# Small softmax vectors moved to the small buffers, and 256 bytes put in front of the query, key and output weights

## The chip, the cores and the metric

The kernel runs on one core of a Trainium2 chip. The metric is the device time of one execution in microseconds (us), launch to end, as the median of several executions.

## What is computed

An input x of 32 batches, 32 tokens each, 512 features, passes through one transformer layer with a per-batch condition. Cut to what matters:

```python
H, KV, HD, HID = 32, 8, 128, 512             # 32 query heads, 8 key/value heads
h = einsum('bct,bcd->bdt', x, W[cond])       # mixes the 32 tokens of a batch
q, k, v = h @ wq, h @ wk, h @ wv             # then rotary embedding on q and k
att = softmax(mask(q @ k.T / sqrt(HD)))      # 32 x 32 scores per batch and head
x = x + (att @ v) @ wo                       # wo: 4096 x 512
y = einsum('bct,bcd->bdt', x, W2[cond])
x = x + quantize(quantize(y) @ qweight.T * scale + bias)
```

All of it is float32. The 1024 rows (32 batches times 32 tokens) are 8 tiles of 128 rows.

## The kernel before

**Precision.** TensorE gets float32 matrices as pairs of "float32r" parts, a high part (`_hi`, made by ScalarE) and what is left over (`_lo`, made by GpSimd or VectorE). `three_pass` multiplies such pairs by three matmuls of 512 columns each into the same PSUM bank; each instruction loads its own 128 x 128 stationary operand:

```python
for i, ((l_hi, l_lo), (r_hi, r_lo)) in enumerate(pairs):
    pe.matmul(dst, l_hi, r_hi, start=(i == 0), stop=False)           # L721
    pe.matmul(dst, l_hi, r_lo, start=False, stop=False)              # L722
    mm = pe.matmul(dst, l_lo, r_hi, start=False, stop=(i == n - 1))  # L723
```

The second argument is stationary (loaded as weights), the third is moving (streamed, 512 float32 values in each partition, 2048 bytes). In a row of the profile, `bank<-A,B` names the moving operand and then the stationary one, without buffer numbers, so `wo7_hi` appears as `wo_hi` and `o2_hi` as `o_hi`.

**Stages.** Everything is written by hand for each engine, and the engines meet only in semaphores. (1) Opening: the conditions are selected, h is computed, and `values` (L693 to L695) computes v for all rows in 16 units of 12 matmuls: units 0 to 7 with `wo_hi`/`wo_lo` as the moving buffers (they hold half of wv then), units 8 to 15 with `o_hi`/`o_lo` as moving buffers. The stationary operand is `hT_hi`/`hT_lo` in all 16. (2) Steady part: for each key/value head g (0 to 7) and each half h (0, 1) of the work, TensorE runs `attend` (small matmuls `p_tr`, `v_st`, L786), `key` (12 matmuls, weights `wk_*`, moving `hT_*`), seven products (`product`, 6 matmuls each, weights `wq_*`, moving `hT_*` or `t_*`: a Strassen-like scheme for two query heads at once), and `project_out` (12 matmuls each for j = 0 to 3, stationary `o_hi`/`o_lo`, moving `wo_hi`/`wo_lo`). In half 1 the small `scores` matmuls (L775) stand between `project_out` j = 2 and j = 3. The heads 2 to 6 are a loop, with g = 0, 1 and 7 written out. (3) Tail: the last projections take other buffers (`wo7_*` moving, `o2_*` or `o_*` stationary), then comes the quantized feed-forward layer in bf16 (L921) with filler matmuls (`hold_clock`, L901).

**Beside TensorE in the steady part.** VectorE (DVE) sums products (`block_sum`, L1021 to L1036), does the two multiplications of the rotary embedding (`rope`, L1045, L1046), softmax (`soft`, L1062 to L1081), the low part of the attention output (`o_low`, L1087) and `accumulate` (L1094), which adds a finished projection to `xacc`. ScalarE (ACT) makes high parts and the half-swapped copy for the rotary embedding (`swap`, L513, L514). GpSimd (POOL) makes low parts of weights and finishes the rotary embedding (`rope_add`, L385). `scores` waits until `rope_add` has finished the fourth query item of the half; `project_out` number n waits until `accumulate` number n - 2 is done.

**Where buffers lie.** `sb` takes the next free bytes of each partition; every buffer begins where the one before it ends, at a multiple of 32 bytes. Buffers of an inner `ExitStack` (`products`, and in it `opening` and `steady`) begin behind those of the outer one. Since nearly all large buffers are multiples of 2048 bytes long, the few small ones set where all that follow begin. This is where the operands of the float32r matmuls begin in a partition, as the remainder of the address divided by 512 (every slice that a matmul takes of them is a whole number of 512 bytes further on):

| buffers | before | after the change |
|---|---|---|
| hT_*, t_*, o_*, o2_*, wo7_* | 64 | 256 |
| wq_*, wk_*, wo_* | 256 | 0 |

So the distance of the stationary operand's start from the moving operand's start, modulo 512, is:

| matmuls | before | after |
|---|---|---|
| products and keys (moving hT, t; stationary wq, wk) | 192 | 256 |
| project_out up to head 6, values units 0 to 7 (moving wo; stationary o, o2, hT) | 320 | 256 |
| values units 8 to 15 (moving o; stationary hT) | 0 | 0 |
| project_out of head 7 (moving wo7; stationary o, o2) | 0 | 0 |

w_sum, s_exp, p_tr and v_st stay where they are. q_rot, k_rot, q_swap, s_nat and the other buffers between hT and o_lo move by 192 bytes together with hT.

Of the kernel before, what the change touches and what calls it, by code (L numbers as in the profile page):

```python
# [7 lines left out]
F32 = mybir.dt.float32  # L8
# [7 lines left out]
P = 128  # L16
# [3 lines left out]
REP = HEADS // KV  # L20
# [5 lines left out]
TPU = TILES // 2  # L26
# [52 lines left out]
def build(nc, x, itok, conds, wq, wk, wv, wo, qweight, w_scale, bias, consts, v_mem, out):  # L79
    with ExitStack() as ctx:  # L80
        def sb(name, shape, dt=F32, area=ctx):
            return area.enter_context(nc.sbuf_tensor(name, shape, dt))
# [10 lines left out]
        y_max = sb("y_max", [P, TILES])  # L93
        f_max = sb("f_max", [P, TILES])
        col = sb("col", [P, 12])
        ones_r = sb("ones_r", [BIAS_ROWS, P], F32R)


        with ExitStack() as products:
            hT_hi = sb("hT_hi", [P, KC, ROWS], F32R, products)  # L100
            hT_lo = sb("hT_lo", [P, KC, ROWS], F32R, products)
            t_hi = sb("t_hi", [P, 4, 2, HALF], F32R, products)
            t_lo = sb("t_lo", [P, 4, 2, HALF], F32R, products)


            with ExitStack() as opening:
                h_full = sb("h_full", [P, KC, ROWS], F32, opening)
                t_full = sb("t_full", [P, 4, 2, HALF], F32, opening)
                selectors = sb("selectors", [P, TILES // 2, 4, 2 * BPT, T], F32, opening)
                wbd1 = sb("wbd1", [P, TILES, BPT, T], F32, opening)  # L110
                wcond = sb("wcond", [P, 4, 2 * T], F32, opening)
                tok_i = sb("tok_i", [P, BATCH], I32, opening)
                tok_f = sb("tok_f", [P, BATCH], F32, opening)
                tok_eq = sb("tok_eq", [P, 4, BATCH], F32, opening)
                warm = sb("warm", [P, 512], BF16, opening)

            with ExitStack() as steady:
                q_rot = sb("q_rot", [P, 2, REP, HALF], F32, steady)
                k_rot = sb("k_rot", [P, 2, HALF], F32, steady)
                q_swap = [sb(f"q_swap{i}", [P, HALF], F32, steady) for i in range(2)]  # L120
                first_p, second_u, third_u = (sb(n, [P, HALF], F32, steady) for n in ("first_p", "second_u", "third_u"))
                s_nat = [sb(f"s_nat{i}", [P, TPU * REP, T], F32, steady) for i in range(2)]
                o_hi = sb("o_hi", [P, TPU, REP * P], F32R, steady)
                o_lo = sb("o_lo", [P, TPU, REP * P], F32R, steady)
                s_max = sb("s_max", [P, TPU * REP], F32, steady)
                s_sum = sb("s_sum", [P, TPU * REP], F32, steady)
                s_rec = sb("s_rec", [P, TPU * REP], F32, steady)
                w_sum = sb("w_sum", [P, 4, 2, HD], F32, steady)
                s_exp = sb("s_exp", [P, TPU * REP, T], F32, steady)
                p_tr = sb("p_tr", [P, TPU * REP, T], F32, steady)  # L130
                v_st = [sb(f"v_st{i}", [P, TPU, HD], F32, steady) for i in range(2)]
                wq_hi = sb("wq_hi", [P, PRODUCTS, 2, HD], F32R, steady)
                wq_lo = sb("wq_lo", [P, PRODUCTS, 2, HD], F32R, steady)
                wk_hi = sb("wk_hi", [P, KC, HD], F32R, steady)
                wk_lo = sb("wk_lo", [P, KC, HD], F32R, steady)
                wo_hi = sb("wo_hi", [P, REP, HID], F32R, steady)
                wo_lo = sb("wo_lo", [P, REP, HID], F32R, steady)
                raw_q = sb("raw_q", [P, 2, KC, 2 * HD], F32, steady)
                raw_k = sb("raw_k", [P, KC, HD], F32, steady)
                raw_o = sb("raw_o", [P, REP, HID], F32, steady)  # L140
# [1194 lines left out]
```

## Time and profile before

| what | value |
|---|---|
| three executions | 546.47, 550.50, 550.77 us; median 550.5 us |
| the profiled execution | 551.23 us, of which its span is 549.4 us |
| busy share of the span: TensorE, VectorE, GpSimd, ScalarE | 94%, 77%, 57%, 46% |
| mean granted share of TensorE's clock | 0.972 |

A row of the profile gives an instruction's start, its duration, and in brackets how long its engine stood idle before it and what ended that. TensorE's instructions overlap, so what one of them costs is not its duration but the distance from its start to the next one's start. Below, that distance is called a step.

### The profile page before, as it was taken

What the parts mean: (1) busy time and instruction counts of PE and PEld (TensorE: products, weight loads), DVE (VectorE), ACT (ScalarE), POOL (GpSimd) and SP (SyncE); (2) the same over time, 40 slices, a digit from 0 to 9 for tenths busy, and PEclk for the clock granted to TensorE, in tenths of its full rate; (3) what the DMA queues carried; (4) which work ended last, traced back from release to release, by engine and by line L of the source; (5) the groups of instructions that cost most, each with busy time, mean ns of one, the idle gap of its engine ahead of it and who ended that gap; (6) DMA issues with size and microseconds to landing.
All of it is one profiled execution on the core that took longest, in us unless ns stands there. A gap on an engine that the chain in (4) does not pass through costs nothing.

```text
span 549.4 us, 9239 instructions
## 1 busy us (share of the span) xinstructions
PE 515.3 (94%) x3150; PEld 407.5 (74%) x3150; DVE 422.1 (77%) x660; ACT 251.2 (46%) x477; POOL 312.6 (57%) x310
## 2 busy tenths in 40 slices
PE   8997999849999999999999999999999999799990
PEld 6886888638787878787888888887878787578530
DVE  5454667696787978797879788887978788765797
ACT  2434256256264636463555446354636453123424
POOL 1247668869838774875688568847884654000002
PEclk9999899978999999999999999999999999989996
DMA  8317311302042022104010401041200023000004
GB/s 262 122 39 245 118 40 38 116 0 58 10 146 57 1 80 75 57 0 153 0 57 0 153 0 57 0 153 34 89 30 20 1 82 116 0 2 1 0 0 153
DMA packets 32644, 35.27 MB, mean 64 GB/s; under 512 B 2251, under 2 KB 22859, under 8 KB 32620
## 3 DMA queue, kind: packets, MB, share of 16 engines
q1 hardware_dynamic: 32620, 34.96, 19.7%
q8 instruction: 14, 0.23, 0.2%
q14 instruction: 10, 0.08, 0.0%
HBM read 28.66 MB, written 6.29 MB: 64 GB/s over the span
## 4 chain that ended last, share of the span: by engine, by line
PE 88%; DVE 5%; POOL 2%; issue 2%; DMA 2%; ACT 1%; SPq 0%; DVEq 0%; ACTq 0%
PE bank L721 24%; PE bank L723 23%; PE bank L722 23%; PE bank L786 3%; PE bank L775 3%; DMA values<-v_st 2%; PE bank L693 2%; PE bank L695 1%; PE bank L694 1%; PE bank L664 1%; PE bank L844 1%; PE bank L921 1%; POOL o_lo L392 1%; PE bank L652 1%; PE bank L901 1%
## 5 line engine op out<-in xcount | busy, mean ns | idle before, releaser
L385 POOL TENSOR_TENSOR q_rot<-q_rot,q_swap 128x512 f32<-128x512 f32 x64 | 88.2, 1378 | 57.9 <-DVE q_swap L1046 57.9
L721 PE MATMUL bank<-wo_hi,o_hi 128*128 128x512 f32 x256 | 103.8, 405 | 3.5 <-issue 3.5
L722 PE MATMUL bank<-wo_lo,o_hi 128*128 128x512 f32 x256 | 102.1, 399 | 0.0
L723 PE MATMUL bank<-wo_hi,o_lo 128*128 128x512 f32 x256 | 102.0, 398 | 0.0
L513 ACT ACTIVATE q_swap<-bank 64x512 f32<-64x512 f32 x80 | 47.6, 596 | 81.7 <-PE bank L723 35.5
L1094 DVE TENSOR_TENSOR xacc<-xacc,bank 128x512 f32<-128x512 f32 x64 | 43.8, 684 | 42.8 <-PE bank L723 42.3
L530 ACT ACTIVATE o_hi<-bank 128x512 fp32r<-128x512 f32 x64 | 33.0, 604 | 73.2 <-PE bank L786 73.2
L721 PEld LDWEIGHTS bank<-wo_hi,o_hi 128*128 128x128 f32 x256 | 48.7, 190 | 17.2 <-issue 5.5
L1046 DVE TENSOR_TENSOR q_swap<-q_swap,cst 128x512 f32<-128x512 f32 x80 | 61.4, 767 | 0.0
L723 PEld LDWEIGHTS bank<-wo_hi,o_lo 128*128 128x128 f32 x256 | 48.8, 191 | 11.9
L722 PEld LDWEIGHTS bank<-wo_lo,o_hi 128*128 128x128 f32 x256 | 48.8, 191 | 10.8
L385 POOL TENSOR_TENSOR k_rot<-k_rot,q_swap 128x512 f32<-128x512 f32 x16 | 20.8, 1298 | 55.4 <-DVE q_swap L1046 55.4
L723 PE MATMUL bank<-t_hi,wq_lo 128*128 128x512 f32 x128 | 50.2, 392 | 0.0
L721 PE MATMUL bank<-t_hi,wq_hi 128*128 128x512 f32 x128 | 50.0, 391 | 0.0
L722 PE MATMUL bank<-t_lo,wq_hi 128*128 128x512 f32 x128 | 50.0, 391 | 0.0
L380 POOL TENSOR_TENSOR wo_lo<-raw_o,wo_hi 128x512 fp32r<-128x512 f32 x32 | 44.9, 1424 | 8.8 <-ACT wo_hi L499 8.8
L371 POOL TENSOR_TENSOR wq_lo<-w_sum,wq_hi 128x256 fp32r<-128x256 f32 x64 | 48.6, 769 | 0.5 <-ACT wq_hi L482 0.5
L514 ACT ACTIVATE q_swap<-bank 64x512 f32<-64x512 f32 x80 | 47.3, 591 | 0.9
L1045 DVE TENSOR_TENSOR q_rot<-bank,cst 128x512 f32<-128x512 f32 x64 | 43.9, 687 | 4.4 <-ACT q_swap L514 2.9
L435 POOL TENSOR_TENSOR xacc<-raw_q,xacc 128x512 f32<-128x512 f32 x2 | 3.1, 1587 | 71.9 <-ACT raw_q L644 71.9
L1087 DVE TENSOR_TENSOR o_lo<-bank,o_hi 128x512 fp32r<-128x512 f32 x64 | 39.6, 681 | 2.2 <-ACT o_hi L530 2.1
L371 POOL TENSOR_TENSOR wq_lo<-raw_q,wq_hi 128x256 fp32r<-128x256 f32 x48 | 38.7, 807 | 0.3
(161 smaller groups left out, 1094.0 us busy)
## 6 DMA issues: line engine op xcount, KB each, us to landing
raw_q<-in_L_attn_wq SPq DMA_DIRECT2D x16, 512.0 KB, 4.1
raw_o<-in_L_attn_wo SPq DMA_DIRECT2D x8, 1024.0 KB, 7.2
v_st<-values SPq DMA_DIRECT2D x16, 256.0 KB, 4.4
xacc<-in_x SPq DMA_DIRECT2D x4, 512.0 KB, 7.5
raw_k<-in_L_attn_wk SPq DMA_DIRECT2D x8, 256.0 KB, 4.4
values<-v_st SPq DMA_DIRECT2D x8, 256.0 KB, 2.0
out<-xacc SPq DMA_DIRECT2D x8, 256.0 KB, 2.0
raw_o<-in_L_attn_wv SPq DMA_DIRECT2D x1, 1024.0 KB, 8.1
```

The lines of the kernel that those rows point to most:

```text
L371: pool.tensor_tensor(wq_lo[:, i], left_part(h, i), wq_hi[:, i].bitcast(F32), ALU.subtract).then_inc(wq_lo_done, 1)
L380: pool.tensor_tensor(lo[:, h, :], raw_o[:, h, :], hi[:, h, :].bitcast(F32), ALU.subtract).then_inc(wo_lo_done, 1)
L385: pool.tensor_tensor(item_out(h, k), item_out(h, k), q_swap[(h + k) % 2][:], ALU.add).then_inc(rope_done, 1)
L513: act.activation(dst[0:P // 2, :], ps[P // 2:P, :], ACT.Copy)
L514: act.activation(dst[P // 2:P, :], ps[0:P // 2, :], ACT.Copy).then_inc(swap_done, 1)
L721: pe.matmul(dst, l_hi, r_hi, start=(i == 0), stop=False)
L722: pe.matmul(dst, l_hi, r_lo, start=False, stop=False)
L723: mm = pe.matmul(dst, l_lo, r_hi, start=False, stop=(i == n - 1))
L1045: dve.tensor_tensor(by_t(item_out(h, k)), by_t(item_ps[k][:]), cos_b, ALU.mult).then_inc(rope_cos, 1)
L1046: dve.tensor_tensor(by_t(q_swap[b][:]), by_t(q_swap[b][:]), sin_b, ALU.mult).then_inc(rope_mul, 1)
L1087: dve.tensor_tensor(by_batch(lo, b), by_tile(ps[b]), by_batch(hi, b).bitcast(F32), ALU.subtract).then_inc(o_lo_done, 1)
L1094: dve.tensor_tensor(xacc[:, tile, :], xacc[:, tile, :], w_ps[j % 2][:], ALU.add).then_inc(acc_done, 1)
```

## The change

Three vectors of 64 bytes in each partition (`s_max`, `s_sum`, `s_rec`) are allocated with the small buffers in front instead of behind `o_lo`, and an unused buffer of 256 bytes, `between`, is put in front of `wq_hi`. The first part pushes everything from `ones_r` to `o_lo` back by 192 bytes and leaves the buffers from `w_sum` to `v_st` where they are; the second pushes `wq_hi` and all behind it back by 256 bytes. No instruction is added, removed or moved on any engine, no semaphore changes; only start addresses differ.

```diff
         col = sb("col", [P, 12])
+        s_max, s_sum, s_rec = (sb(n, [P, TPU * REP]) for n in ("s_max", "s_sum", "s_rec"))
         ones_r = sb("ones_r", [BIAS_ROWS, P], F32R)
...
                 o_lo = sb("o_lo", [P, TPU, REP * P], F32R, steady)
-                s_max = sb("s_max", [P, TPU * REP], F32, steady)
-                s_sum = sb("s_sum", [P, TPU * REP], F32, steady)
-                s_rec = sb("s_rec", [P, TPU * REP], F32, steady)
                 w_sum = sb("w_sum", [P, 4, 2, HD], F32, steady)
                 s_exp = sb("s_exp", [P, TPU * REP, T], F32, steady)
                 p_tr = sb("p_tr", [P, TPU * REP, T], F32, steady)
                 v_st = [sb(f"v_st{i}", [P, TPU, HD], F32, steady) for i in range(2)]
+                sb("between", [P, 64], F32, steady)
                 wq_hi = sb("wq_hi", [P, PRODUCTS, 2, HD], F32R, steady)
                 wq_lo = sb("wq_lo", [P, PRODUCTS, 2, HD], F32R, steady)
```

## Rows read from the trace of the kernel before

**Rows 1.** The page: TensorE's busy time; the chain that ended last, by engine.

```profile
PE 515.3 (94%) x3150; PEld 407.5 (74%) x3150; DVE 422.1 (77%) x660; ACT 251.2 (46%) x477; POOL 312.6 (57%) x310
...
PE 88%; DVE 5%; POOL 2%; issue 2%; DMA 2%; ACT 1%; SPq 0%; DVEq 0%; ACTq 0%
```

**Rows 2.** Stretches: us, length, TensorE busy (instructions), granted clock, DMA share, GB/s.

```profile
123.00:126.40 3.40, 3.40 (x12) 0.50 0.21 36
126.40:475.30 348.90, 348.67 (x2262) 1.00 0.18 56
475.30:478.95 3.65, 0.43 (x2) 0.89 0.00 0
478.95:485.00 6.05, 6.05 (x14) 0.50 0.00 0
```

**Rows 3.** Timeline, TensorE: project_out, 36 matmuls; start us, duration.

```profile
268.02 0.40 PE L722 MATMUL bank<-wo_lo,o_hi 128*128 128x512 f32 x1
...
276.19 0.39 PE L721 MATMUL bank<-wo_hi,o_hi 128*128 128x512 f32 x1
```

**Rows 4.** Timeline, TensorE: first matmul of the seven products, first of project_out.

```profile
258.18 0.39 PE L721 MATMUL bank<-hT_hi,wq_hi 128*128 128x512 f32 x1
...
267.79 0.39 PE L721 MATMUL bank<-wo_hi,o_hi 128*128 128x512 f32 x1
```

**Rows 5.** Timeline, TensorE: values, units 2 and 3, second and last matmul.

```profile
26.41 0.39 PE L694 MATMUL bank<-wo_lo,hT_hi 128*128 128x512 f32 x1
...
31.54 0.39 PE L695 MATMUL bank<-wo_hi,hT_lo 128*128 128x512 f32 x1
```

**Rows 6.** Timeline, TensorE: values, units 8 and 9, the last 14 matmuls.

```profile
47.06 0.39 PE L694 MATMUL bank<-o_lo,hT_hi 128*128 128x512 f32 x1
...
50.01 0.39 PE L695 MATMUL bank<-o_hi,hT_lo 128*128 128x512 f32 x1
```

**Rows 7.** Timeline, TensorE: head 7's project_out, 13 settled matmuls; then 11 after a restart.

```profile
487.12 0.39 PE L723 MATMUL bank<-wo_hi,o_lo 128*128 128x512 f32 x1
...
489.84 0.39 PE L723 MATMUL bank<-wo_hi,o_lo 128*128 128x512 f32 x1
...
496.14 0.40 PE L722 MATMUL bank<-wo_lo,o_hi 128*128 128x512 f32 x1
...
498.45 0.39 PE L723 MATMUL bank<-wo_hi,o_lo 128*128 128x512 f32 x1
```

**Rows 8.** Timeline, TensorE: bf16 matmuls of 512 columns, four and three.

```profile
523.36 1.04 PE L921 MATMUL bank<-wT,y 128*128 128x512 bf16 x4
524.23 0.81 PE L901 MATMUL bank<-w 128*128 128x512 bf16 x3
```

**Rows 9.** Groups by line, TensorE, 126.5 to 475 us; count, busy, mean ns.

```profile
L721 PE MATMUL bank<-wo_hi,o_hi 128*128 128x512 f32 x224 | 89.4, 399 | 0.2 <-issue 0.2
L721 PE MATMUL bank<-t_hi,wq_hi 128*128 128x512 f32 x104 | 40.6, 390 | 0.0
L721 PE MATMUL bank<-hT_hi,wq_hi 128*128 128x512 f32 x78 | 30.4, 390 | 0.0
L722 PE MATMUL bank<-hT_lo,wk_hi 128*128 128x512 f32 x50 | 19.7, 395 | 0.0
```

**Rows 10.** Timeline, half 1 of a loop turn: VectorE, GpSimd, TensorE.

```profile
236.91 0.70 DVE L1026 TENSOR_TENSOR bank<-bank,first_p 128x512 f32<-128x512 f32 x1 [0.59 <-PE bank L723]
...
245.51 0.68 DVE L1094 TENSOR_TENSOR xacc<-xacc,bank 128x512 f32<-128x512 f32 x1
...
247.60 1.67 POOL L385 TENSOR_TENSOR q_rot<-q_rot,q_swap 128x512 f32<-128x512 f32 x1 [0.63 <-DVE q_swap L1046]
...
246.43 0.40 PE L721 MATMUL bank<-wo_hi,o_hi 128*128 128x512 f32 x1
...
249.33 0.75 PE L775 MATMUL bank<-q_rot,k_rot 128*32 128x128 f32 x20
```

**Rows 11.** Timeline, half 0: accumulate on VectorE, and project_out j = 2.

```profile
219.87 0.68 DVE L1094 TENSOR_TENSOR xacc<-xacc,bank 128x512 f32<-128x512 f32 x1
...
221.54 0.39 PE L721 MATMUL bank<-wo_hi,o_hi 128*128 128x512 f32 x1
```

**Rows 12.** Timeline around the two long idle stretches of TensorE.

```profile
121.02 2.09 PE L786 MATMUL bank<-p_tr,v_st 32*128 32x128 f32 x32 [7.26 <-DVE p_tr L1081]
...
475.77 0.69 DVE L1094 TENSOR_TENSOR xacc<-xacc,bank 128x512 f32<-128x512 f32 x1 [1.62 <-PE bank L723]
476.37 2.48 DVE L1087 TENSOR_TENSOR o_lo<-bank,o_hi 128x512 fp32r<-128x512 f32 x4
...
478.95 0.77 PE L721 MATMUL bank<-wo_hi,o_hi 128*128 128x512 f32 x1 [3.22 <-issue]
```

## The prediction

> **What bounds the kernel now.** I read the page first. TensorE is busy for 94% of the span, and 88% of the chain that ended last is TensorE's own work [rows 1]. The table of stretches says where: from 126.4 to 475.3 us, 348.9 us long, TensorE is busy for 348.67 us at the full clock [rows 2]. Nothing but a shorter TensorE program, or shorter steps of the same program, can shorten that stretch. The change leaves the program alone. So the only question is whether start addresses set how long a step is.
>
> They seem to. I took steps from the timeline, always as a difference of two starts divided by the number of matmuls between, in stretches at full clock without a wait:
>
> - project_out: 276.19 - 268.02 = 8.17 us over 35 matmuls, **0.2334 us** [rows 3].
> - products: 267.79 - 258.18 = 9.61 us over 42, **0.2288 us** [rows 4].
> - values with wo moving: 31.54 - 26.41 = 5.13 us over 22, **0.2332 us** [rows 5].
> - values with o moving: 50.01 - 47.06 = 2.95 us over 13, **0.2269 us** [rows 6].
> - head 7's project_out, settled: 489.84 - 487.12 = 2.72 us over 12, **0.2267 us** [rows 7].
> - bf16 matmuls of the same 512 columns: 524.23 - 523.36 = 0.87 us over 4, 0.2175 us [rows 8].
>
> The reader should see two pairs. The two kinds of values units have the same shape, the same stationary buffers and the same accumulation, and differ by 6.3 ns a step. Ordinary project_out and head 7's are the same function on other buffers and differ by 6.7 ns. In both pairs the faster one is the one whose moving and stationary operands start at the same remainder (64 and 64), and the slower one has 256 against 64. The products, with 64 against 256, lie between. All float32r steps are longer than the bf16 ones. I call the distance from the moving operand's start to the stationary one's start the phase: phase 0 costs 0.2267, phase 192 costs 0.2288, phase 320 costs 0.2333.
>
> One more row speaks for two streams that disturb each other, and not for a price on a start address by itself: right after other work head 7's stream takes 498.45 - 496.14 = 2.31 us over 10 steps, 0.231 each, and settles at 0.2267 only later, with addresses that never change in remainder [rows 7]. A settling-in needs something relative between the read of the moving operand and the load of the next weights.
>
> **The change part by part.** No instruction, wait or transfer is added, removed or moved; the softmax vectors themselves are read and written by the same VectorE instructions wherever they lie, which I cost at nothing. The 192 bytes of the first part and the 256 of the second change the phases: 192 and 320 both become 256, and 0 stays 0.
>
> Phase 256 occurs in no float32r row. Phases in this kernel differ by multiples of 512 within one kind of matmul without any effect (the 42 products all fall into one stream at 0.2288), so the pattern repeats after 512 bytes or a part of 512. It does not repeat after 128, since 192 and 320 would then be the same phase, yet they cost 0.2288 and 0.2333. What is left is 256 or 512. If it is 256, phase 256 is phase 0 and costs 0.2267. If it is 512, phase 256 is unknown, between its neighbours 192 and 320 by position, but nothing excludes values outside: below down to the 0.2175 of bf16, above by as much as the spread seen so far. I take 0.2267, since a repeat after 256 with 192 as "minus 64" and 320 as "plus 64" uses only values that the rows show; it is nearest to the clean pair of values units [rows 5, 6].
>
> The sum, for the stretch 126.4 to 475.3:
>
> 1. project_out: 224 matmuls on each of the three lines [rows 9], 670 in all (the other two lines have 223). 670 x (0.2333 - 0.2267) = 4.4 us.
> 2. products: 104 + 78 on each of three lines, 546 in all; keys: about 50 on each, 149 in all [rows 9]. 695 x (0.2290 - 0.2267) = 1.6 us.
> 3. Settling-in: after each attend and each scores the stream starts anew. At phase 0 that costs 10 x (0.231 - 0.2267) = 0.04 us [rows 7]; with 13 attends and 7 scores in this stretch, 20 x 0.04 = 0.9 us comes off the gain.
> 4. What the other engines allow. In half 1 of a loop turn VectorE waits for TensorE's fourth product, starts at 236.91 [rows 10], and from there its own work, ScalarE's and GpSimd's are a chain that ends with GpSimd's last rope_add at 247.60 + 1.67 = 249.27; scores starts at 249.33, at once behind it [rows 10]. TensorE itself arrives there only just in time: from the fourth product it has 18 product matmuls and 36 of project_out, 18 x 0.2288 + 36 x 0.2333 = 12.52 us. These would shrink to 54 x 0.2267 = 12.24 us, and the 0.28 us saved turn into a wait in front of scores. The same chain also holds project_out j = 2, which starts at 246.43 while the accumulate it needs ends at 245.51 + 0.68 = 246.19; that wait would be inside the other one, not beside it. This is so in the five loop turns: 5 x 0.28 = 1.4 us is lost. In half 0 the corresponding accumulate ends at 219.87 + 0.68 = 220.55 and project_out j = 2 starts at 221.54 [rows 11], so 1 us of room is left and the gain passes.
>
> 4.4 + 1.6 - 0.9 - 1.4 = 3.7 us. Outside the stretch: before 121 us the wait of 7.26 us for VectorE's p_tr [rows 12] swallows most of what products and keys of the first heads save; with some 160 of them at 2.3 ns and about half on the path I count 0.2 us. Values with wo moving save 8 x 12 x 6.5 ns = 0.6 us of TensorE time, but the chain there goes through ScalarE, GpSimd and a DMA, so I count nothing; it would be 0.6 if that cover were gone. Head 7's stream keeps its phase: 0. The idle stretch of 3.22 us before 478.95 starts with the end of a projection, goes through accumulate and four o_low on VectorE (475.77 to 478.85) and stays as it is [rows 12]; the gain in front of it passes whole.
>
> Total 3.9 us. The profiled execution, 551.23 us (549.4 of span and 1.8 around it), would become 547.3. It lies 0.7 us above the median of 550.5, so the median should come to 546.6; I say **546.8 us**. The clock moves single executions by as much: it stood at half in two stretches, each right behind an idle one [rows 2, 12], and one of the three executions is 4 us below the others.
>
> **A rule that speaks against it.** The table of stretches shows steps that depend on buffers at the same full clock [rows 3, 5, 6]. The Trainium skill says otherwise: "TensorE: Matmul & The Clock Gate", section "Step-by-step: what each phase is for", states that TensorE has two independent read ports and that "loading the next tile's weights doesn't steal SBUF read bandwidth from the running matmul". By that rule the phase would have no price and the time would stay 550.5 us. Those two kinds of values units, 6.3 ns apart with one operand the same, disagree with it unless something else than the phase tells the buffers apart.
>
> **The rivals.**
>
> - *No change by a repeat after 512.* If phase 256 costs what lies midway between 192 and 320, 0.231, project_out saves 670 x 2.2 ns = 1.5 us and products and keys lose 695 x 2.1 ns = 1.5 us: **550.5 us**. The same time results if the phase is not the cause at all and the buffers differ by something that the change leaves alone. For it: no row shows phase 256. Against it: the order 0, 192, 320 fits a repeat after 256 as well.
> - *Slower: the price is on the starts, not on their distance.* A moving operand at 0 modulo 256 would cost 6.4 ns more than one at 64 [rows 5, 6], weights at 0 modulo 256 another 2.1 [rows 4, 6]. After the change both are at 0 modulo 256 everywhere, a step would be 0.2267 + 0.0064 + 0.0021 = 0.2352 us. The 670 lose 1.9 ns each (1.3 us), the 695 lose 6.4 ns (4.4 us), the first heads and the late values units some 250 x 6.5 ns = 1.6 us, head 7's 96 matmuls 8.5 ns each (0.8 us). TensorE-bound stretches pass this on whole: 8.1 us, **558.6 us**. It decides from the point where 64 is a good start for both operands and 0 for neither. For it: the rows of before fit it as exactly as they fit the phase. Against it: the settling-in [rows 7].
> - *More: phase 256 is the far side of a pattern of 512 bytes and the two streams miss each other.* A step would be near the bf16 one. With 17 ns on project_out and 12 on products and keys, and everything between the fourth product and scores lost again, a loop turn saves 60 x 17 + 90 x 12 ns = 2.1 us; 6.7 turns give 14 us: **536.5 us**. For it only: nothing excludes it.
>
> **How the numbers follow.** The sum above 0.52, no change 0.20, slower 0.16, more 0.10, anything else 0.02. The forecast is the first one's, 546.8 us. Its own range is 543.5 to 549.5 (the wait before scores lost or not, 1.4 us, the settling-in 0.9 us, and the clock's luck on a median). The range for 8 in 10 takes in no change with its scatter and reaches part of the way to the outer two: 540 to 556. Within 1% of 550.5 is 545.0 to 556.0, about what a measurement here can tell from no change. Below 545.0 lies all of "more" and a third of the first case: 0.28. Above 556.0 lies the slower rival, nearly whole: 0.15. Within: 0.57.
>
> **What would show it.** In the profile after, a step of project_out and of the products taken as above should both be 0.2267; steps of head 7 and of late values unchanged. In half 1, a wait of about 0.3 us in front of scores should appear behind GpSimd's rope_add, and none in half 0. If products are above 0.233 the starts themselves have the price; if all is near 0.231 the pattern repeats after 512; if steps are near 0.216 the third rival holds, and the waits behind VectorE and GpSimd are then much longer than 0.3 us. The forecast is wrong, too, if GpSimd's and VectorE's own instructions change their durations with the addresses, of which I have no row.

## The result, and the profile after

| | before | after |
|---|---|---|
| median of the compared executions | 549.91 us (20) | 545.99 us (20) |
| lowest, highest | 545.75, 551.18 | 543.20, 551.53 |
| span of the profiled execution | 549.4 us | 545.9 us |
| mean granted clock of it | 0.972 | 0.972 |

The ratio is 0.9932, with a 95% interval of 0.9911 to 0.9954: the change makes the kernel 0.7% faster, and no change lies outside the interval. The forecast of 546.8 us against 550.5 is a ratio of 0.9933. Executions far above the others of their kernel (551.45 and 551.53 us here; of the runs below 553.11 of `early_add`, and 1311.8 of the kernel before beside `late_lows`) count in the medians but not in the ratios; without the first two the median after is 545.06 us. Single executions of either kernel are spread over 5 to 8 us, and much of that goes with the granted clock: of the kernel before, those beside `late_lows` that took 545.9 to 547.6 us had a mean clock of 0.980 to 0.984, and those that took 549.7 to 552.0 us 0.969 to 0.975; one of 552.97 us had 0.981. So I take the causes from the two profiled executions, whose stretches at half clock lie at the same places.

The page after: busy times, and the chain that ended last by engine.

```profile
PE 510.5 (94%) x3150; PEld 406.4 (74%) x3150; DVE 423.7 (78%) x660; ACT 251.0 (46%) x477; POOL 311.3 (57%) x310
...
PE 37%; POOL 28%; issue 23%; DVE 6%; DMA 2%; ACT 1%; POOLq 1%; SPq 0%; DVEq 0%; ACTq 0%
```

TensorE has the same 3150 instructions and is 4.8 us less busy than in [rows 1]; VectorE is 1.6 us busier. The chain tells something else than it seems to: TensorE's share falls from 88% to 37%, although it is busy for 94% as before. The chain is followed back to whatever released an instruction, and GpSimd now releases TensorE a little late once in each loop turn; from there it stays on GpSimd's chain for long. A share of this chain shows who is last, not by how much.

The stretch that answers to [rows 2], with the busy time of TensorE, weight loads, VectorE, ScalarE and GpSimd, then clock, DMA share and GB/s:

```profile
126.40:471.96 345.56, 344.71 (x2263) 279.73 (x2261) 287.24 (x440) 173.78 (x335) 235.24 (x232) 1.00 0.18 56
```

348.90 us have become 345.56.

The steps, from the timeline of TensorE: the first products, then the first two and the last of the 24 matmuls of project_out that answer to [rows 3, 4]; values, units 2 and 3, as [rows 5]; head 7 as [rows 7].

```profile
26.65 0.39 PE L693 MATMUL bank<-wo_lo,hT_hi 128*128 128x512 f32 x1
...
31.43 0.39 PE L693 MATMUL bank<-wo_lo,hT_hi 128*128 128x512 f32 x1
...
256.88 0.39 PE L720 MATMUL bank<-hT_hi,wq_hi 128*128 128x512 f32 x1
...
266.40 0.39 PE L720 MATMUL bank<-wo_hi,o_hi 128*128 128x512 f32 x1
266.62 0.39 PE L721 MATMUL bank<-wo_lo,o_hi 128*128 128x512 f32 x1
...
271.61 0.39 PE L722 MATMUL bank<-wo_hi,o_lo 128*128 128x512 f32 x1
...
483.60 0.39 PE L722 MATMUL bank<-wo_hi,o_lo 128*128 128x512 f32 x1
...
486.32 0.39 PE L722 MATMUL bank<-wo_hi,o_lo 128*128 128x512 f32 x1
```

Products: 266.40 - 256.88 = 9.52 us over 42, 0.2267 us a step (before 0.2288). project_out: 271.61 - 266.62 = 4.99 us over 22, 0.2268 (before 0.2334). Values with wo moving: 4.78 us over 21, 0.2276 (before 0.2332). Head 7: 2.72 us over 12, 0.2267, and 2.31 us over 10 behind a restart (from 492.62 us on), both the same as before. The duration that a row shows, 0.39 or 0.40, hardly tells these apart, since the ends of matmuls are modelled; the distance of starts does.

Where the time went is seen in attend, which comes once in each half of a loop turn. Its starts:

| attend at the end of | before | after | gain so far |
|---|---|---|---|
| first head | 121.02 | 120.71 | 0.31 |
| | 150.52 | 149.88 | 0.64 |
| half 0 | 175.40 | 174.33 | 1.07 |
| half 1 | 202.36 | 201.37 | 0.99 |
| half 0 | 227.24 | 225.82 | 1.42 |
| half 1 | 254.21 | 252.92 | 1.29 |
| ... | | | |
| last three | 458.59 | 455.45 | 3.14 |
| | 471.56 | 468.23 | 3.33 |
| | 490.16 | 486.64 | 3.52 |

A half 0 took 24.87 us and takes 24.45: it gains 0.42. A half 1 took 26.97 and takes 27.02 to 27.11: it gains nothing and loses 0.05 to 0.14. Both run the same shorter steps, so in half 1 something else is last.

Timeline after, half 1 of the turn whose rows of before are [rows 10]: TensorE from its attend, VectorE, GpSimd, then TensorE around the two places where it waits.

```profile
225.82 0.39 PE L785 MATMUL bank<-p_tr,v_st 32*128 32x128 f32 x4
...
229.74 2.47 DVE L1086 TENSOR_TENSOR o_lo<-bank,o_hi 128x512 fp32r<-128x512 f32 x4
...
238.72 1.20 DVE L1045 TENSOR_TENSOR q_swap<-q_swap,cst 128x512 f32<-128x512 f32 x1
...
241.03 1.28 DVE L1045 TENSOR_TENSOR q_swap<-q_swap,cst 128x512 f32<-128x512 f32 x1
...
244.23 0.68 DVE L1093 TENSOR_TENSOR xacc<-xacc,bank 128x512 f32<-128x512 f32 x1
...
233.49 1.30 POOL L384 TENSOR_TENSOR k_rot<-k_rot,q_swap 128x512 f32<-128x512 f32 x1 [2.51 <-DVE q_swap L1045]
234.74 2.54 POOL L379 TENSOR_TENSOR wo_lo<-raw_o,wo_hi 128x512 fp32r<-128x512 f32 x2
...
239.31 1.20 POOL L370 TENSOR_TENSOR wq_lo<-raw_q,wq_hi 128x256 fp32r<-128x256 f32 x1
240.47 1.29 POOL L384 TENSOR_TENSOR q_rot<-q_rot,q_swap 128x512 f32<-128x512 f32 x1
...
246.33 1.67 POOL L384 TENSOR_TENSOR q_rot<-q_rot,q_swap 128x512 f32<-128x512 f32 x1 [0.64 <-DVE q_swap L1045]
...
244.50 0.39 PE L722 MATMUL bank<-wo_hi,o_lo 128*128 128x512 f32 x1
244.97 0.50 PE L720 MATMUL bank<-wo_hi,o_hi 128*128 128x512 f32 x1
...
247.59 0.39 PE L722 MATMUL bank<-wo_hi,o_lo 128*128 128x512 f32 x1
248.05 0.41 PE L774 MATMUL bank<-q_rot,k_rot 128*32 128x128 f32 x6
```

project_out j = 2 starts 244.97 - 244.50 = 0.47 us behind its predecessor instead of 0.23, once VectorE's accumulate has ended (244.23 + 0.68 = 244.91). Scores starts 0.46 us behind its predecessor, at once behind rope_add (246.33 + 1.67 = 248.00); where nothing holds it, that distance is 0.32. The table of waits of the weight loads, 126.4 to 472 us, says the same (us in total, times, longest):

```profile
PEld bank L774 <- POOL q_rot L384: 2.8, 6, 0.5
PEld bank L720 <- DVE xacc L1093: 2.4, 5, 0.5
```

Before, the second of these did not occur. From attend to scores half 1 took 249.33 - 227.24 = 22.09 us before and takes 248.05 - 225.82 = 22.23 us. The rows show what lies between: attend's result is split by VectorE's four o_low (229.74 to 232.21), behind them come the keys' rope products and GpSimd's add of them (233.49), and from there GpSimd works without a gap through two wo_low and four q_low to its first late rope_add at 240.47.

One link of this chain is longer than before. The addition of the mask to the scores (L1062 before, L1061 after), which reads two SBUF operands, stands ahead of the four o_low on VectorE; timeline of VectorE before, then after:

```profile
227.95 0.69 DVE L1062 TENSOR_TENSOR s_nat<-s_nat,cst 128x512 f32<-128x512 f32 x1
...
226.53 0.88 DVE L1061 TENSOR_TENSOR s_nat<-s_nat,cst 128x512 f32<-128x512 f32 x1
```

It takes 0.88 us instead of 0.69. Attend comes earlier now, GpSimd's queue does not: its sum for the next weights (L363) runs from 226.12 to 226.86 and so over the start of this addition, where before it had ended at 227.19 + 0.74 = 227.93, ahead of it. The first o_low starts 3.92 us behind attend, before 3.73. In the five halves 1 of the loop this instruction takes 0.68 to 0.69 us in the kernel before and 0.84 to 0.88 in the kernel after.

The long idle stretch in front of the last project_out is unchanged, 3.22 us as in [rows 12]:

```profile
475.57 0.77 PE L720 MATMUL bank<-wo_hi,o_hi 128*128 128x512 f32 x1 [3.22 <-issue]
```

### The profile page after: what moved, and what is told of

Same layout as the page of the kernel before. It is cut to its first block, busy times and chain, and to the rows that moved or that the text cites. A ratio compares the mean times of both kernels' runs of the same rounds, so it can differ in the third digit from the quotient of the medians.

```text
span 545.9 us, 9239 instructions
## 1 busy us (share of the span) xinstructions
PE 510.5 (94%) x3150; PEld 406.4 (74%) x3150; DVE 423.7 (78%) x660; ACT 251.0 (46%) x477; POOL 311.3 (57%) x310
## 4 chain that ended last, share of the span: by engine, by line
PE 37%; POOL 28%; issue 23%; DVE 6%; DMA 2%; ACT 1%; POOLq 1%; SPq 0%; DVEq 0%; ACTq 0%
POOL q_rot L384 9%; POOL wq_lo L370 8%; PE bank L720 8%; PE bank L721 8%; PE bank L722 8%; POOL wo_lo L379 5%; DMA values<-v_st 2%; PE bank L692 2%; PE bank L694 1%; PE bank L693 1%; PE bank L785 1%; POOL w_sum L360 1%; PE bank L663 1%; POOL w_sum L363 1%; PE bank L843 1%
## 5 line engine op out<-in xcount | busy, mean ns | idle before, releaser
L721 PE MATMUL bank<-wo_lo,o_hi 128*128 128x512 f32 x256 | 100.8, 394 | 0.0
L722 PE MATMUL bank<-wo_hi,o_lo 128*128 128x512 f32 x256 | 100.7, 393 | 0.0
```

## The experiments

Two questions were put to the chip. What property of the addresses sets the step: the distance of the two starts (the phase) modulo 256, the same modulo 512, or the starts themselves? And what is last in half 1? Phases of products and of project_out are each other's negatives here, since hT_hi and o_hi stay and wq and wo move together. In the kernels made from the kernel after by another size of `between`, one of the two operands always starts at 0 modulo 256 (hT and o at 256), so each phase from 32 to 224, except 128, is tried with one pair of starts only. A median holds more or less of the half clock by luck, so steps and halves from the profile decide and times stand beside them.

### One part of the change at a time

`vectors_only` is the kernel after without its 256 bytes:

```diff
                 v_st = [sb(f"v_st{i}", [P, TPU, HD], F32, steady) for i in range(2)]
-                sb("between", [P, 64], F32, steady)
                 wq_hi = sb("wq_hi", [P, PRODUCTS, 2, HD], F32R, steady)
```

> The kernel after without the 256 bytes in front of wq_hi: only the softmax vectors are moved. All float32r operands then start at 256 modulo 512, so the distance of starts (phase) is 0 modulo 512 everywhere. Theory A, the step depends on the phase modulo 256: steps of 0.2267 us in project_out, products and keys, time as the kernel after, ratio to before 0.993. Theory B, the pattern repeats after 512 bytes and the 256 bytes matter: steps differ from 0.2267 in products or project_out, time between before and after. Theory C, the price is on the start of an operand by itself, and 0 modulo 512 is good for weights where 256 is not: products back near 0.2288.

`between_only` is the kernel before with this line alone:

```diff
                 v_st = [sb(f"v_st{i}", [P, TPU, HD], F32, steady) for i in range(2)]
+                sb("between", [P, 64], F32, steady)
                 wq_hi = sb("wq_hi", [P, PRODUCTS, 2, HD], F32R, steady)
```

> The kernel before with only the 256 bytes in front of wq_hi; the softmax vectors stay. Phase of products and keys 448 instead of 192, of project_out 64 instead of 320. Theory A (repeat after 256): nothing changes, products 0.2288, project_out 0.2333, ratio to before 1.000. Theory B (repeat after 512): steps change in at least one of the two. Theory C (starts by themselves): weights at 0 instead of 256 modulo 512 are better, products faster than 0.2288.

`vectors_only`: 546.46 us (12 executions), ratio 0.9937 (0.9902 to 0.9972). Timeline of TensorE, first product, then first, second and last matmul of project_out:

```profile
258.68 0.39 PE L719 MATMUL bank<-hT_hi,wq_hi 128*128 128x512 f32 x1
...
268.20 0.39 PE L719 MATMUL bank<-wo_hi,o_hi 128*128 128x512 f32 x1
268.43 0.39 PE L720 MATMUL bank<-wo_lo,o_hi 128*128 128x512 f32 x1
...
273.41 0.39 PE L721 MATMUL bank<-wo_hi,o_lo 128*128 128x512 f32 x1
```

9.52 us over 42 and 4.98 over 22: 0.2267 and 0.2264, at phase 0. `between_only`: 550.59 us (10), ratio 1.0009 (0.9971 to 1.0047), the same places:

```profile
255.55 0.39 PE L722 MATMUL bank<-hT_hi,wq_hi 128*128 128x512 f32 x1
...
265.17 0.39 PE L722 MATMUL bank<-wo_hi,o_hi 128*128 128x512 f32 x1
265.40 0.39 PE L723 MATMUL bank<-wo_lo,o_hi 128*128 128x512 f32 x1
...
270.53 0.39 PE L724 MATMUL bank<-wo_hi,o_lo 128*128 128x512 f32 x1
```

9.62 us over 42 and 5.13 over 22: 0.2290 and 0.2332, as before. So 256 bytes change nothing, in either direction, and the whole gain comes from moving hT and what follows it by 192 bytes. A repeat after 512 only is refuted, and with it the need for the second part of the change.

### Swapping the two phases, and the curve between

`phase64` has 320 bytes in place of 256, so that products come to phase 64 and project_out to 192:

```diff
-                sb("between", [P, 64], F32, steady)
+                sb("between", [P, 80], F32, steady)
```

> The kernel after with 320 instead of 256 bytes in front of wq_hi: wq, wk, wo start at 64 modulo 512, the rest stays at 256. Modulo 256 the products now have the phase that project_out had before (64) and project_out has the one that products had before (192). Theory A: products and keys 0.2333, project_out 0.2288 us a step; loop and rest lose 695 x 6.6 ns + 670 x 2.1 ns = 6 us of TensorE time against the kernel after, of which what now waits in half 1 is covered; ratio to before about 1.000 to 1.003. Theory C: a weights start at 64 modulo 256 is what the fast streams of before had, products stay at 0.2267 or near it, and project_out, with its moving operand at 64, too.

Timeline of TensorE, the same places:

```profile
256.23 0.40 PE L720 MATMUL bank<-hT_hi,wq_hi 128*128 128x512 f32 x1
...
266.03 0.40 PE L720 MATMUL bank<-wo_hi,o_hi 128*128 128x512 f32 x1
266.26 0.39 PE L721 MATMUL bank<-wo_lo,o_hi 128*128 128x512 f32 x1
...
271.31 0.39 PE L722 MATMUL bank<-wo_hi,o_lo 128*128 128x512 f32 x1
```

Products 9.80 us over 42, 0.2333; project_out 5.05 over 22, 0.2295. The two have changed places: products now have the step that project_out had, and the other way round. Other buffers, other data and another kind of matmul show the same step once they start at the same places: moving at 256 and stationary at 64 modulo 512 costs 0.2333, be it project_out before or the products here. This does not yet tell the distance from the pair of starts, since both are what is exchanged. The distance itself is tested where one phase occurs with several pairs: phase 0 costs 0.2267 with both operands at 64 (head 7 before), with both at 256 (`vectors_only`) and with 256 and 0 (the kernel after), and phase 128 has two pairs, below. The time, 548.46 us (10), ratio 0.9993 (0.9958 to 1.0027), is no change, and the steps ask for that: one kind of matmul lost about what the other gained. No wait stands in front of scores in half 1.

Three further sizes, one execution each: 288 bytes (`[P, 72]`, products at 32, project_out at 224), 352 (`[P, 88]`, 96 and 160), 384 (`[P, 96]`, 128 and 128).

> The kernel after with 288 bytes in front of wq_hi: phase 32 modulo 256 for products and keys, 224 for project_out. The theory that the phase modulo 256 sets the step says only that the pair (products, project_out) is one curve of the phase: known are 0: 0.2267, 64: 0.2333, 192: 0.2289. Smooth, it gives 32: 0.230 and 224: 0.228. The theory that the start itself counts says nothing of 32. Either step below 0.2267 would be a better place than the kernel after has.

> The kernel after with 352 bytes in front of wq_hi: phase 96 modulo 256 for products and keys, 160 for project_out. On a smooth curve 96 lies at or above 0.2333 and 160 at or above 0.2289; if the curve has its maximum at 128, both are higher than at 64 and 192.

> The kernel after with 384 bytes in front of wq_hi: phase 128 modulo 256 for products, keys and project_out alike. If the phase alone sets the step, products and project_out must show the same step, whatever it is; a difference of over 1 ns between them would show that something else of the buffers counts.

They took 552.23, 551.57 and 550.62 us. First product and first matmul of project_out with `phase32`:

```profile
258.99 0.40 PE L720 MATMUL bank<-hT_hi,wq_hi 128*128 128x512 f32 x1
...
268.79 0.40 PE L720 MATMUL bank<-wo_hi,o_hi 128*128 128x512 f32 x1
```

9.80 us over 42, 0.2333. From all kernels, by mean settled steps:

| phase modulo 256 | 0 | 32 | 64 | 96 | 128 | 160 | 192 | 224 |
|---|---|---|---|---|---|---|---|---|
| ns a step | 226.7 | 233.3 | 233.3 | 234.3 | 232.4 to 232.7 | 233.2 | 228.9 to 229.4 | 233.3 |

I had expected a smooth curve, 230 at 32 and 228 at 224: wrong. It is a plateau near 233 with a deep hole at 0 and a shallower one at 192. At 128 both kinds of matmul have the same phase from different starts (products: moving at 0, stationary at 128 modulo 256; project_out the other way round), and they have nearly the same step (232.4 and 232.7), as the distance asks for. At 64 and 192 no second pair was tried. Of these eight, 0 is the best. Phases between multiples of 32 were not tried.

### What is last in half 1

GpSimd's first late rope_add starts at 240.47, behind its own work, while the sine product that it needs on VectorE had ended at 238.72 + 1.20 = 239.92. My first theory: GpSimd's order holds the chain, and one add ahead of one q_low frees it. `early_add`, on the kernel after:

```diff
+                first = 4 if h == 0 else 3
                 if more:
-                    for i in range(4):
+                    for i in range(first):
                         q_low(*follow, i)
-                for k in range(1, 5):
+                rope_add(g, h, 1)
+                if more:
+                    for i in range(first, 4):
+                        q_low(*follow, i)
+                for k in range(2, 5):
                     rope_add(g, h, k)
```

> The kernel after, with GpSimd's order changed in half 1 alone: the rotary add of the second item is put in front of the fourth low part of wq instead of behind it. If GpSimd's queue holds what TensorE waits for in half 1 (in the profile after: 0.21 us in front of project_out j = 2, 0.14 us in front of scores, in each of 5 loop turns), these waits shrink by 0.2 us or more a turn and the time falls by 1 to 1.7 us, ratio to before 0.990 to 0.991. If VectorE's own work is what sets the chain, the waits stay and the time is that of the kernel after, 0.993.

547.02 us (12), ratio 0.9957 (0.9918 to 0.9996); half 1 takes 27.09 us, as after. Only the sizes of the two waits changed: project_out j = 2 starts 247.77 - 247.38 = 0.39 us behind its predecessor instead of 0.47, and scores 0.53 instead of 0.46. In the table of waits of the weight loads those at j = 2 come to 2.1 us in five times, after 2.4. The rows of VectorE's first and third sine product of a query item, of GpSimd, and of project_out j = 2:

```profile
241.59 1.20 DVE L1050 TENSOR_TENSOR q_swap<-q_swap,cst 128x512 f32<-128x512 f32 x1
...
246.05 1.07 DVE L1050 TENSOR_TENSOR q_swap<-q_swap,cst 128x512 f32<-128x512 f32 x1
...
242.87 1.30 POOL L384 TENSOR_TENSOR q_rot<-q_rot,q_swap 128x512 f32<-128x512 f32 x1 [0.62 <-DVE q_swap L1050]
...
245.28 1.28 POOL L384 TENSOR_TENSOR q_rot<-q_rot,q_swap 128x512 f32<-128x512 f32 x1
...
247.77 0.50 PE L725 MATMUL bank<-wo_hi,o_hi 128*128 128x512 f32 x1
```

The add no longer waits behind GpSimd's own work but for VectorE (0.62 us), and VectorE's first and third sine product take 1.20 and 1.07 us. The second, at 243.91, takes 0.81 instead of 1.28, and the third 1.07 instead of 0.68: what was gained at one was lost at the next. The shortest instructions of that line take 0.68 (one stands in the rows of `late_lows` below). So GpSimd's order alone is not the theory. The second one: a sine product, which reads two SBUF operands, is stretched when a GpSimd instruction that reads SBUF, a q_low or a rope_add, is running as it starts. The 1.20 us belong to a q_low (it ends at about 242.25, the sine product 0.54 us later), the 1.07 us to the rope_add at 245.28, which ends at 246.56 and the sine product at 247.12. The Trainium skill, "SBUF — State Buffer", section "Who interferes with whom", states this of a VectorE instruction with two SBUF inputs and a GpSimd instruction that reads SBUF; these rows agree, and a q_low that starts while a sine product runs takes 1.20 us itself (at 239.31 in the rows after) against 0.74 elsewhere.

Two kernels on this. `spread_add` has two q_low ahead of the adds and one behind each of the first two:

```diff
+                first = 4 if h == 0 else 2
                 if more:
-                    for i in range(4):
+                    for i in range(first):
                         q_low(*follow, i)
                 for k in range(1, 5):
                     rope_add(g, h, k)
+                    if more and first + k - 1 < 4:
+                        q_low(*follow, first + k - 1)
```

> The kernel after, with GpSimd's order changed in half 1 alone: only two low parts of wq stand in front of the rotary add of the second item, and the other two stand behind the second and the third item's add. In the run before, VectorE's product with the sine (two operands in SBUF) took 1.20 us instead of 0.68 because it stood still until GpSimd's third low part had ended. If that collision sets the chain, it goes now: the add of item 1 starts 0.5 us earlier, the waits of TensorE in half 1 shrink from 0.35 us (kernel after) to below 0.1 us a turn, and the time falls by 1.3 to 1.8 us against the kernel after, ratio to before 0.990. If the chain is VectorE's own sum of work, the waits stay at 0.3 us or more and the ratio at 0.993.

544.64 us (12), ratio 0.9941 (0.9907 to 0.9975), half 1 26.95 us: some of it, not all; no wait is left at j = 2, but scores stands 0.70 us behind its predecessor. Timeline, VectorE and GpSimd:

```profile
240.83 1.08 DVE L1048 TENSOR_TENSOR q_swap<-q_swap,cst 128x512 f32<-128x512 f32 x1
...
238.91 1.20 POOL L370 TENSOR_TENSOR wq_lo<-w_sum,wq_hi 128x256 fp32r<-128x256 f32 x1
240.06 1.29 POOL L384 TENSOR_TENSOR q_rot<-q_rot,q_swap 128x512 f32<-128x512 f32 x1
```

The first two sine products take 0.68 and 0.80 us now, the third and the fourth 1.08. What meets the third is not the q_low, which had ended at 240.11, but the rope_add from 240.06 to 241.35. The q_low had been stretched to 1.20 us by the second sine product and so pushed this rope_add back; the same happens once more at the fourth.

`late_lows` moves the two behind all four adds:

```diff
+                first = 4 if h == 0 else 2
                 if more:
-                    for i in range(4):
+                    for i in range(first):
                         q_low(*follow, i)
                 for k in range(1, 5):
                     rope_add(g, h, k)
                 if more:
+                    for i in range(first, 4):
+                        q_low(*follow, i)
                     if h == 1:
                         k_low(g + 1)
```

`before_late_lows` is the same edit on the kernel before, and `after_again` the kernel after once more, beside them on the same chip.

> The kernel after, with two low parts of wq in half 1 moved behind all rotary adds of GpSimd. In the two runs before, each low part that stood between the adds made VectorE's product with the sine take 1.1 to 1.2 us instead of 0.68, and the wait before scores only changed its place. If these collisions set the chain in half 1, all are gone now: no wait before scores or project_out j = 2, the time from one attend to the next in half 1 falls from 27.05 us (kernel after) to about 26.55 (24.45 of half 0 and 2.1 for scores), 2.5 us in five turns, ratio to before 0.988 to 0.989. If the chain is VectorE's own sum of work, 27.0 us stays and the ratio is 0.993.

> The kernel before with the same two low parts moved. There TensorE waits only 0.01 to 0.03 us for the rotary add, since its own longer steps fill the time: if the phase is what shortens TensorE's program and the collisions only set what can be had of it, this does next to nothing by itself: half 1 at 26.95 us, ratio 0.9995 to 1.000.

> The changed kernel once more, on the same chip as the kernel with the late low parts: ratio to before 0.993 and half 1 at 27.05 us.

| | median us (executions) | ratio to before | half 1, us |
|---|---|---|---|
| before | 549.72 (24) | | 26.97 |
| after_again | 544.78 (12) | 0.9944 (0.9912 to 0.9976) | 27.09 |
| before_late_lows | 549.21 (12) | 1.0007 (0.9971 to 1.0043) | 26.96 |
| late_lows | 542.30 (7) | 0.9911 (0.9876 to 0.9946) | 26.56 |

Timeline of `late_lows`, half 1: attend, the first two sine products, the first and the last rope_add, the end of project_out and scores, the next attend.

```profile
224.94 0.39 PE L788 MATMUL bank<-p_tr,v_st 32*128 32x128 f32 x4
...
237.84 0.68 DVE L1048 TENSOR_TENSOR q_swap<-q_swap,cst 128x512 f32<-128x512 f32 x1
...
239.64 0.81 DVE L1048 TENSOR_TENSOR q_swap<-q_swap,cst 128x512 f32<-128x512 f32 x1
...
238.60 1.30 POOL L384 TENSOR_TENSOR q_rot<-q_rot,q_swap 128x512 f32<-128x512 f32 x1 [0.81 <-DVE q_swap L1048]
...
244.46 1.68 POOL L384 TENSOR_TENSOR q_rot<-q_rot,q_swap 128x512 f32<-128x512 f32 x1 [0.62 <-DVE q_swap L1048]
...
246.35 0.39 PE L725 MATMUL bank<-wo_hi,o_lo 128*128 128x512 f32 x1
246.67 0.32 PE L777 MATMUL bank<-q_rot,k_rot 128*32 128x128 f32 x4
...
251.50 0.39 PE L788 MATMUL bank<-p_tr,v_st 32*128 32x128 f32 x4
```

The sine products take 0.68 and 0.81 us, the first late add starts 238.60 - 224.94 = 13.66 us behind attend (after: 240.47 - 225.82 = 14.65), and both waits are gone: the last add ends at 246.14, before project_out does, and scores follows it at the free distance of 0.32 us. Half 1 now gains 26.97 - 26.56 = 0.41 us, as half 0 does. On the kernel before the same edit moves nothing that can be measured, since TensorE itself was the last to arrive at scores. Between the two kernels with this edit the change of the addresses is worth 545.1 - 540.3 = 4.8 us by the spans of the profiled executions (6.9 by the medians, which hold the clock too); a half 0 gains 0.42 us and a half 1 0.40, where without the edit a half 1 gained nothing.

So `late_lows` beats both kernels. The ratio has the interval of few executions and overlaps that of `after_again`; but six of its seven executions (542.10 to 543.32) lie below the lowest of the twelve of `after_again` (543.59), and half 1 is 0.53 us shorter in each loop turn. The expected ratio, 0.988 to 0.989, lies inside the interval, the value measured above it.

The rows say what the edit removes. In the kernel after and in `late_lows` alike VectorE starts its sum of the fourth product 9.6 us behind attend and has from there no gap above 0.11 us up to its last sine product, which starts 19.75 us behind attend in the one and 18.75 in the other. The four sine products take 1.20, 1.28, 0.68 and 0.68 us in the one and 0.68, 0.81, 0.68 and 0.69 in the other, 0.98 us less, and the last rope_add starts 20.51 and 19.52 us behind attend. So the stretched products account for the whole difference; GpSimd's order counts through what it lets collide with them, and `early_add`, which only let the first add go ahead, moved a collision and gained nothing. One collision is left in every kernel here: the last rope_add takes 1.67 us, where the others take 1.3, beside a softmax product of VectorE with two SBUF operands (L1073 after, at 246.17). No run moved that one.

## Why the prediction was right, and where a step of it failed

- *A step is set by the phase, and the pattern repeats after 256.* Right, and shown: `vectors_only` and `between_only` separate 0 from 256 and 192 from 448 and find them equal; `phase64` exchanges the steps of the two kinds of matmul with their starts. That it is the distance, and not the pair of starts, is shown at phases 0 and 128; at 64 and 192 it is taken over from there. The reasoning from before (0 at 0.2267, 192 at 0.2288, 320 at 0.2333) held. That 64 and 192 lie on a slope on both sides of 0 was only my picture, and the curve refutes it; the forecast did not need it.
- *project_out, 4.4 us, and products with keys, 1.6 us.* The mean settled steps after are 227.0, 226.7 (products) and 227.2 ns (keys), where 226.7 was forecast: right within 0.5 ns, 0.3 us of the sum. (They come to 226.7 ns in all three when the first ten steps behind each restart are left out.) The sum took 0.2290 for products and keys, where the rows gave 0.2288 for the products; that is 0.1 us.
- *Half 1 loses 0.28 us in a turn.* This step failed in size and in its anchor. It took the chain to start at TensorE's fourth product, which would itself come earlier with shorter steps. The chain starts at attend and goes through o_low, the keys' add and GpSimd's own work, in which of TensorE's steps only the keys' occur; attend to scores stayed at 22.1 to 22.2 us whatever TensorE saved in between. VectorE does sum the fourth product 0.08 us earlier behind attend (9.59 instead of 9.67), but the first sine product cannot end before GpSimd's third q_low does, which it meets: it is stretched to 1.20 us (before 0.96) and ends 14.10 us behind attend, before 13.94. So half 1 loses all of its 0.42 us, and about 0.08 more, since o_low and with it GpSimd's queue come later behind attend by the 0.19 us of the stretched addition of the mask: 0.5 a turn, 2.5 us in five turns, where 1.4 was forecast. "That wait would be inside the other one, not beside it" held for the time: the trace shows two waits, 0.24 us at j = 2 and 0.14 before scores, but scores starts when the last rope_add ends, however many waits lie before. Together with the slower steps behind the first they are the 0.50 us by which TensorE would have been early: scores starts 22.23 us behind attend, and 21.73 in `late_lows`, where nothing holds it. In `spread_add` the first wait is gone and the second is 0.38.
- *Settling-in, 0.9 us.* From the first head's attend to the restart behind the idle stretch the gain is (478.95 - 475.57) - 0.31 = 3.1 us. With 6.0 us of shorter steps and 2.5 lost in half 1, some 0.4 us is left for settling-in. I work this out backwards and have not measured it: it was put too high by about 0.5 us, and so hid nearly half of the error of the step above. One reason is that the sum charges the whole of it to the kernel after, while the keys behind attend settle in before the change too: their mean step is 229.9 ns before, against the products' 228.8, and 228.8 after, against 226.7.
- *Half 0 passes the gain, first heads 0.2 us, head 7 and the idle stretch unchanged.* Right: 0.42 us a half; 0.31 us at 121; 0.2267 and 3.22 us as before.
- *Values, nothing.* The step shortens to 0.2276, and the gain at the first head's attend is 0.31 us in all, so at most a part of 0.6 us arrived.
- *The sum.* The span of the profiled execution fell by 3.5 us, forecast 3.9; the median by 3.9. The mechanism was right; that the number was met so closely is luck in part, since 1.1 us too little loss in half 1 and 0.5 us too much settling-in stand against each other, and since a median moves by some us with the clock (545.99 with all 20 executions, 545.06 with 18).
- *The rivals.* No change by a repeat after 512: refuted by `between_only`. A price on each start by itself: refuted, since products and project_out are at 0.2267 in the kernel after and not at 0.2352. `phase64` does not speak against it: with 6.4 ns for a moving operand at 0 modulo 256 and 2.1 for a stationary one it, too, gives 0.233 and 0.229 there. Streams that miss each other at 256: refuted, 256 is 0. The rule of the Trainium skill ("TensorE: Matmul & The Clock Gate", section "Step-by-step: what each phase is for") that loading the next weights takes no read bandwidth from the running matmul would leave the time at 549.9 us; project_out with the same data at 0.2333 and 0.2267, by the starts alone, disagrees with that forecast for float32r. Whether it is the read bandwidth that the loads take is another matter: that the two reads collide in SBUF is the explanation I would give, and it is only argued, since no run shows the weight load and the stream separately.

## What to carry to other kernels

Measure the step of a long float32r matmul stream as the distance of starts, and lay the buffers out so that stationary and moving operand start at the same remainder modulo 256: here that was worth 2.8% of a step of project_out and 0.9% of one of the products, for no instruction. When the engine that bounds the kernel gets faster, follow each stage's other engines from the last point that does not move with it (here attend), not from the nearest wait: what they have queued there eats the gain. Work of GpSimd that reads SBUF and is not urgent belongs behind the stretch in which VectorE's two-operand instructions are on the path; here that was worth 0.53 us a loop turn once TensorE's steps were short, and nothing before.

## What the runs showed of the hardware

- The step of a 512-column float32r matmul is 226.7 ns at phase 0 and 228.9 to 234.3 ns at the seven other multiples of 32 modulo 256, with no smooth path between: 32 and 224, the closest tried to 0, cost 233.3 both. Phases 0 and 128 were seen with more than one pair of starts, the others with one pair modulo 256 each.
- A stream at phase 0 reaches 226.7 ns only after about ten steps, which take 231 on average (head 7, 2.31 us over 10).
- A VectorE product of two SBUF operands of 128x512 takes 0.68 us alone and up to 1.20 us beside a GpSimd subtraction (q_low) or 1.07 to 1.28 us beside a GpSimd addition (rope_add), both of which read SBUF. The other way round, a q_low that starts while such a product runs takes 1.20 us in place of 0.74.
- The same VectorE instruction, the addition of the mask, takes 0.68 to 0.69 us in the loop's halves 1 before and 0.84 to 0.88 after: a shift in time against GpSimd changed what it costs. VectorE's whole busy time does not show this alone, since it is 422.1 us before, 423.7 after and 423.6 in `between_only`, whose steps are those of before.
